# Spline coefficients on GpSimd, gathers at other places of its queue, one convolution tap on ScalarE, and two buffers for the feed block's input

## The reference

```python
xn = layernorm(x)
q = silu(causal_conv4(xn @ Wq)); k = silu(causal_conv4(xn @ Wk)); v = silu(causal_conv4(xn @ Wv))
beta = sigmoid(xn @ Wb); g = -exp(A_log) * softplus(xn @ Wa + dt_bias)
# 6 heads, keys of 64, values of 128; q and k are l2-normed
for t in tokens:
    S = S * exp(g[t]); delta = (v[t] - k[t] @ S) * beta[t]
    S = S + outer(k[t], delta); o[t] = q[t] @ S
attn = (o * rsqrt(mean(o*o) + eps) * norm_weight * silu(xn @ Wg)) @ Wo
gate_w, up_w, down_w = (catmull_rom(control_points, ...) for each)   # 2048x512, 2048x512, 512x2048
ffn = (silu(xn @ gate_w.T) * (xn @ up_w.T)) @ down_w.T
out = x + attn + ffn
```

## Time and profile before

| | |
|---|---|
| span of the profiled execution | 890.5 us |
| mean granted TensorE clock | 0.944 |
| busy: PE / DVE / ACT / POOL | 781.9 / 585.2 / 470.9 / 358.4 us |
| share of the span | 88% / 66% / 53% / 40% |
| DMA | 62.22 MB, mean 70 GB/s |

### The profile page before, as it was taken

The page is one execution under the profiler, slowest core; times in us unless marked ns, Lnnn a source line. Parts: engine busy times, 40 slices in busy tenths (PEclk is TensorE's granted clock), DMA queues, the critical chain, the costliest instruction groups (busy, mean ns, idle before and its releaser), DMA issues. The chain is left out here.

```text
span 890.5 us, 15471 instructions
## 1 busy us (share of the span) xinstructions
PE 781.9 (88%) x5688; PEld 454.6 (51%) x5688; DVE 585.2 (66%) x1425; ACT 470.9 (53%) x1078; POOL 358.4 (40%) x384
## 2 busy tenths in 40 slices
PE   2979388895988999997899997898687999999998
PEld 1455166553635774655675654664233444444443
DVE  4799958757894787796778897566593444444400
ACT  3756746462685565486666487566672333333300
POOL 3385911365795554667364768022231000000000
PEclk9989699898997999899999999999699999999999
DMA  6502010141003123003013001054695232231011
GB/s 197 198 13 51 13 61 10 65 118 37 7 1 93 45 85 94 13 1 115 7 60 112 25 1 33 6 162 104 169 186 153 72 94 85 60 82 48 25 52 44
DMA packets 60081, 62.22 MB, mean 70 GB/s; under 512 B 30535, under 2 KB 45244, under 8 KB 60006
## 3 DMA queue, kind: packets, MB, share of 16 engines
q1 hardware_dynamic: 53526, 44.97, 18.0%
q0 software_dynamic: 4224, 13.11, 5.0%
q10 hardware_dynamic: 2256, 3.15, 1.0%
HBM read 33.69 MB, written 19.73 MB: 60 GB/s over the span
## 5 line engine op out<-in xcount | busy, mean ns | idle before, releaser
L581 PE MATMUL bank<-x_parts,w 128*128 128x512 f16 x576 | 130.1, 384 | 1.5 <-DVE x_parts L942 1.5
L1971 DVE TENSOR_TENSOR hh<-sg,pu 128x512 f32<-128x512 f32 x64 | 43.9, 686 | 96.8 <-ACT sg L1942 78.8
L581 PEld LDWEIGHTS bank<-x_parts,w 128*128 128x128 f16 x576 | 56.2, 99 | 69.8 <-issue 7.0
L1863 POOL DMA_DIRECT2D yr<-y_attn x16 | 8.7, 544 | 186.7 <-DMA out<-yr 186.7
L581 PE MATMUL bank<-w,x_parts 128*128 128x384 f16 x384 | 75.7, 354 | 8.5 <-ACT V L1359 6.0
L1942 ACT ACTIVATE sg<-pg 128x512 f32<-128x512 f32 x64 | 38.0, 594 | 77.7 <-PE pg L1894 77.1
L581 PEld LDWEIGHTS bank<-w,x_parts 128*128 128x128 f16 x384 | 38.7, 106 | 39.3 <-issue 8.8
L1568 POOL TENSOR_TENSOR rn<-t,mhalf 128x6 f32<-128x6 f32 x16 | 22.7, 1417 | 89.1 <-DVE t L1148 89.1
L985 DVE SCALAR_TENSOR_TENSOR cv<-raw,taps,cv 128x512 f32<-128x512 f32 x72 | 55.1, 832 | 0.0
L1907 PE MATMUL pd<-dw,it 128*128 128x512 f16 x128 | 48.8, 381 | 0.0
L1908 PE MATMUL pd<-dw,it 128*128 128x512 f16 x128 | 48.6, 380 | 0.0
(11 more groups left out here) (293 smaller groups left out, 2050.1 us busy)
## 6 DMA issues: line engine op xcount, KB each, us to landing
xb<-in_x SPq DMA_DIRECT2D x4, 1024.0 KB
xr<-in_x SPq DMA_DIRECT2D x16, 256.0 KB, 2.6
y_attn<-xr SPq DMA_DIRECT2D x16, 256.0 KB, 2.0
down_rows<-inv SPq DMA_DIRECT2D x8, 512.0 KB
yr<-y_attn POOLq DMA_DIRECT2D x16, 256.0 KB, 2.9
out<-yr SPq DMA_DIRECT2D x16, 256.0 KB, 2.7
xn_hi<-x_parts POOLq DMA_DIRECT2D x4, 512.0 KB
xn_lo<-x_parts POOLq DMA_DIRECT2D x4, 512.0 KB
```

The costliest lines, as they stand in the source:

```text
L581: ins = nc.tensor.matmul(out, a, b, start=first and i == 0, stop=last and i == 2)
L1971: v.tensor_tensor(hh[:, i % 2, :], sg[:, i % 2, :], pu[i % 2][:], ALU.mult).then_inc(h_ready, 1)
```

## The change

The arithmetic stays the same; engines and places in their queues change.

- `Cubics` on DVE becomes `PoolCubics` on POOL: 30 linked steps and a last one, since POOL has only operations with two tensors here, so a factor is a tensor or a sum. They stand behind the W copies of supertile 0. (The old class stays for the down weights' coefficients.)
- The 16 gathers: of those in the q/k part of supertile 1 none is left; 0 to 7 stand beside the recurrence of supertile 0 and directly behind it, 8 to 15 behind the W copies of supertile 1 (before: 12 to 15), each waiting for the one before. SP's stores move with them.
- The present tap of q and k (the fourth) becomes an ACT operation (`present_tap`) that starts `cv`; DVE adds the other three.
- For supertiles 1 to 3 POOL clears `tin`, ahead of nk, and DVE no longer does.
- In the tail, `project_out` of the last chunk stands behind feature 5 instead of ahead of it, and `og_part` ahead of `turned_low`.
- x of the feed block has two places. x(1) is loaded ahead of the last move, x(2) at the block's start, x(3) behind the moves of the first supertile.

```diff
+    def slopes(self, pool):
...
+        link(pool, tt(out=self.frac[:, 1, :], in0=self.frac[:, 0, :], in1=self.one, op=ALU.subtract))
+        link(pool, tt(out=t1, in0=p1, in1=p2, op=ALU.subtract))
+        link(pool, tt(out=t2, in0=p3, in1=p0, op=ALU.subtract))
+        link(pool, tt(out=t2, in0=t2, in1=half, op=ALU.mult))
...
+    def shifted(self, pool):
...
+        link(pool, tt(out=t1, in0=c3, in1=self.u, op=ALU.mult))
+        link(pool, tt(out=t2, in0=t1, in1=t1, op=ALU.add))
...
+        g.tensor_copy(d3, c3).then_inc(self.step, 1)
...
-            ready(pe, ("WO", NCH - 2), b)
-            project_out(b, NCH - 1)
             start.features(pe, s0, 5, bank[1])
             ready(pe, ("AU", NCH - 1, 1), b)
             start.turn(pe, 2, bank[6], P.ident)
+            ready(pe, ("WO", NCH - 2), b)
+            project_out(b, NCH - 1)
...
-                for i in range(TAPS):
+                for i in range(TAPS - 1):
...
-                            if not (s.first() and n < 2):
-                                dve.wait_ge(silu_done, s.val(NBLK, n - 1))
-                        src = raw[:, n % 3, i:i + ST]
-                        out = cv[:, n % 2, :]
-                        w = P.taps[:, n, i:i + 1]
-                        if i == 0:
-                            ins = v.tensor_scalar(out, src, w, None, ALU.mult)
+                            dve.wait_ge(last_tap, s.val(NQK, n + 1))
                         else:
                             dve.wait_ge(dve_step, last[n])
-                            ins = v.scalar_tensor_tensor(out=out, in0=src, scalar=w, in1=out, op0=ALU.mult, op1=ALU.add)
...
-                if not s.first():
-                    dve.wait_ge(downs.down_stored, 32 * s.idx())
-                if s.idx() >= 2:
-                    dve.wait_ge(samples.kept, 16 * (s.idx() - 1))
-                dve.wait_ge(t32_step, step(v.memset(tin, 0.0)))
-                cleared = step(v.memset(tin[:, 0:SUB * SUB:SUB + 1], 1.0))
...
-                if b.first() and c == 0:
-                    dve.wait_ge(samples.ctrl_in, 48)
-                    samples.cubics.slopes(dve)
-                if b.first() and c == 1:
-                    samples.cubics.shifted(dve)
...
+                og_part(b, NCH - 1)
                 start.turned_low(dve, 0, bank[4])
-                og_part(b, NCH - 1)
                 start.feature_lo(dve, s0, 4, bank[0])
                 start.turned_low(dve, 1, bank[5])
-                residual(b, NCH - 1)
                 start.feature_lo(dve, s0, 5, bank[1])
                 start.turned_low(dve, 2, bank[6])
+                residual(b, NCH - 1)
...
+            def present_tap(s, n):
+
+                ready(act, ("blk", n), s)
+                if s.first() and n == 0:
+                    act.wait_ge(prep.small_in, prep.SMALL)
+                if not (s.first() and n < 2):
+                    act.wait_ge(silu_done, s.val(NBLK, n - 1))
+                sc.activation(cv[:, n % 2, :], raw[:, n % 3, TAPS - 1:], ACT.Copy, scale=P.taps[:, n, TAPS - 1:TAPS]
+                              ).then_inc(last_tap, 1)
...
                 for n in range(NQK):
                     raw_out(s, n)
+                    if n < 2:
+                        present_tap(s, n)
...
                     if n >= 2:
                         silu(s, n - 2)
+                        present_tap(s, n)
...
+                if not s.first():
+                    pool.wait_ge(downs.down_stored, 32 * s.idx())
+                    if s.idx() >= 2:
+                        pool.wait_ge(samples.kept, 16 * (s.idx() - 1))
+                    g_.memset(tin, 0.0).then_inc(tin_cleared, 1)
+                    pool.wait_ge(tin_cleared, s.val(2, 1))
+                    g_.memset(tin[:, 0:SUB * SUB:SUB + 1], 1.0).then_inc(tin_cleared, 1)
...
+                if s.first():
+                    pool.wait_ge(samples.ctrl_in, 48)
+                    samples.cubics.slopes(pool)
+                    samples.cubics.shifted(pool)
                 if s.idx() == 1:
-                    samples.gather(pool, range(12, IB), paced=True)
+                    samples.gather(pool, range(8, IB), paced=True)
...
                 if b.first():
-                    if c == NCH - 1:
-                        samples.gather(pool, range(1, 3))
+                    if c >= 1:
+                        samples.gather(pool, range(2 * c - 1, 2 * c))
...
                 norm_scale(b, 0)
+                if r == 0:
+                    samples.gather(pool, range(0, 1))
                 for c in range(1, NCH - 1):
                     beside(b, c)
                     norm_scale(b, c)
-                if r == 0:
-                    samples.gather(pool, range(0, 1))
+                    if r == 0:
+                        samples.gather(pool, range(2 * c, 2 * c + 1))
                 spill(s)
                 beside(b, NCH - 1)
                 norm_scale(b, NCH - 1)
                 pool.wait_ge(og_ready, b.val(NCH, NCH))
                 downs.low(pool, NCH * b.idx() + NCH - 1)
                 if r == 0:
-                    samples.gather(pool, range(3, 4))
+                    samples.gather(pool, range(6, 8))
...
-                if r == 0:
-                    samples.store_rows(sp)
+                    if r == 0 and c == 0:
+                        samples.store_rows(sp)
+                        samples.group(sp, range(0, 1))
                 for c in range(NCH - 2):
+                    if r == 0:
+                        samples.group(sp, range(2 * c + 1, 2 * c + 3))
                     store_y(b, c)
                     load_residual(b, c + 2)
...
-            for n in range(5, NP):
+            for n in range(5, NP - 1):
                 start.move(sp, s0, n)
+            start.load_x(sp, At(None, 1))
+            start.move(sp, s0, NP - 1)
...
-            start.load_x(sp, At(None, 1))
+            start.load_x(sp, At(None, 2))
...
-                if s < nst - 2:
-                    start.load_x(sp, At(None, s + 2))
+                if s < nst - 3:
+                    start.load_x(sp, At(None, s + 3))
...
-        if not s.first():
-            sp.wait_ge(self.feat_made, s.val(NP, 0))
-        sp.dma_start(self.x_hi.rearrange("p b c -> p (b c)"), self.scr.xh[s.idx()]).then_inc(self.x_in, 16)
-        sp.dma_start(self.x_lo.rearrange("p b c -> p (b c)"), self.scr.xl[s.idx()]).then_inc(self.x_in, 16)
+        if s.idx() == 1:
+            sp.wait_ge(self.turned_made, self.TURNS)
+        elif s.idx() >= 2:
+            sp.wait_ge(self.feat_made, s.val(NP, 0) - NP)
```

117 lines of the change are left out of this document (84 added, 33 removed).

## The result

Over 20 executions each, the kernel before takes a median of 899.5 us and the changed one 893.0, which is 6.5 less. The ratio of the two is given as 0.9905, with a 95% interval of 0.988 to 0.993, a gain of 8.5 us: it goes by executions in the chip's faster state alone, and leaves out four of the changed kernel. Forecast were 872 and a gain of 21.7. The kernel is faster, as forecast, but gains far less, and 893.0 lies above the range of 861 to 885.

What follows compares the result with a forecast made beforehand. PE was taken as the busiest engine, held up by others in the long stretches. Terms -7.8 - 6.7 + 7.9 - 5.2 + 0 - 2.2 - 7.7 = -21.7 from 892.5 gave 870.8, plus 1.2 towards the median: 872, range 861 to 885.

Steps and rivals of the forecast that it cites:

- Bound and reading: Whole kernel: PE busiest but held up by others in the long stretches; total built on the profiled execution of 892.5 us.
- Coefficients, -7.8: Recurrence beside supertile 0: cubic coefficients moved from DVE to POOL at 0.72 a step save 7.8 us net.
- the 1.9 for a late rn: Recurrence beside supertile 0: rn, queued behind POOL's coefficient steps, is done at 144.3 instead of 142.4, giving 1.9 us back.
- the "about 45": Recurrence beside supertile 0: the changed profile would show it at about 45 us, DVE waiting 2 for rn of chunk 0.
- Gathers out of the q/k part, and taps there, -8.0: Supertile 1's q/k part: removing POOL's gathers saves 6.7 us net, the present tap on ScalarE 1.3.
- Eight gathers, +7.9: Behind supertile 1's W copies: four more gathers, 2.73 us each, make the rows late, costing 7.9 us after 3.0 of slack.
- Present tap, -5.2: q/k parts of four supertiles: the tap moved from DVE to ScalarE saves 1.3 us each, 5.2 in all.
- rival 4: Supertile 0's solve and recurrence: POOL and DVE hold each other up, 0.7 per POOL operation, +20 us, total 892; 10%.
- Clearing on POOL, 0: Inversion's matrix cleared by POOL instead of DVE: 0 us, or +1.6 if POOL's pause before block 6's halo is gone.
- tail, -2.2: Attention's tail: og_part earlier and feature 5 ahead of the product save 2.2 us, half of 4.3, since moves may delay feature 6.
- Two places for x, -7.7: Feed: PE's three waits for x and 1.6 us of half clock go, 9.1 less 1.4, saving 7.7 us.
- "I leave 1.4 for them": Feed: allowance of 1.4 us, out of 9.1, for down-row gathers that POOL still issues while PE waits for x.

Runs made afterwards that it cites:

- e3: Changed kernel with feed's x(2) and x(3) loaded behind moves 2 and 3 of a supertile instead of ahead of them: median 889.2 us.
- e7: Changed kernel with feed's loads of x back in their old places, the two places kept: median 889.8 us, ratio 0.9895 to the kernel before.
- e9: Changed kernel with POOL's first v tap sum in supertile 0 held until VectorE's down-weight coefficient steps are done: median 887.0 us.
- e4: Changed kernel with the present tap of q and k back on VectorE: median 894.2 us, ratio 0.9905 to the kernel before.
- e2: Changed kernel with gathers 8 to 11 taken back ahead of the masks of chunks 2 and 3 in supertile 1: median 879.9 us.
- e12: Changed kernel with the edits of e2, e9 and e3 and four down gathers under way in feed: median 871.6 us, ratio 0.963 to the kernel before.
- e5: Kernel before, unaltered, profiled a second time in a single execution: 906.6 us, span 904.6.

## Why the prediction was wrong, point by point

- **Bound and reading.** Right for the stretches it named: both irregular ones are gone. Wrong in its base: one execution, of 892.5, was taken for the kernel, and its median of three moved the time by 1.2. The median of 20 is 7.0 above it. With the forecast's own terms 878 would have come out of the right level, which is still 15 too low.
- **Coefficients, -7.8.** Right in mechanism and step price (0.61 to 0.74 against 0.72). The stage gained 11.5 on the mean of the two executions before, and the clock in it rose from 0.84 and 0.90 to 1.00. That the 1.9 for a late rn did not come back is luck: the inversion was late for another reason (below), which gave POOL 1.7 of slack. Where the recurrence could start at 129.6 to 130.9 (e3, e7, e9; 134.8 and 136.0 in the changed kernel's own executions), DVE waits 1.1 to 1.6 behind POOL's steps and the recurrence takes 45.2 to 45.7, the "about 45" of the forecast.
- **Gathers out of the q/k part, and taps there, -8.0.** -9.0 measured; e4 gives the tap 2.1 of it, so the gathers 6.9. (The forecast's 7.8 less 1.0 is 6.8, not the 6.7 it has.)
- **Eight gathers, +7.9.** The mechanism was right and shown by e2; from the inversion on, the stage lost 9.4 on the mean of both executions before, 11.5 on the one used. In parts: the rows came 30.7 behind the last W copy where the terms give 29.4, rn began 9.2 later than before (37.7 behind that copy, 28.5 before), and 2.3 more went behind it, at half clock (288.8 to 305.9), which the term had in its bound only.
- **Present tap, -5.2.** The q/k parts gained as forecast (1.9 in supertile 0, 2.1, 1.0, 1.0). The step that failed is that the gain would shift along behind it. In supertile 0 it ran into a chain on DVE that starts when its data lands (73.5 to 73.9 in every execution, whatever came before), so at least the 1.9 was given back. And POOL's v taps, which come earlier too, meet that chain: five and seven of its steps were held in the two executions, one and four in the kernel before, some 1.0 each, and the stage is 5.2 longer on the means of two. Over nine executions of this code it is 3.3 longer, with one to seven held steps. That held steps delay the inversion is shown (it follows the chain's end by 3.2 throughout, and e9 and e12 have no held step); that the tap makes them more frequent is only likely. It is rival 4's mechanism, at a place and from a part that the prediction had not looked at; at the place it named, three short sums on DVE were held and nothing else.
- **Clearing on POOL, 0; tail, -2.2.** The way into feed is 2.4 shorter; ACT waits 2.62 for a move ahead of feature 6, the tile it has to wait for, as the prediction has it. Of what was changed on the way into feed only x(1) was tried alone (e7: it gives nothing there), and the clearing not at all.
- **Two places for x, -7.7.** The step that failed, and the largest: "I leave 1.4 for them". The three waits for x went, but the down gathers behind them came even later: feed's supertiles 0 to 2 gained nothing (158.0 before and 160.2 changed, on the means of two), and e7 without the early loads is no slower. The rows that would have told it were there, in the kernel before:

```profile
637.16 1.09 POOL L1867 DMA_INDIRECT dw<-down_rows,member  x1 [22.65 <-DMA member<-in_member]
...
673.71 0.94 POOL L1867 DMA_INDIRECT dw<-down_rows,member  x1 [1.69 <-DMA dw<-down_rows,member]
...
679.53 0.38 PE L1907 MATMUL pd<-dw,it 128*128 128x512 f16 x1
```

  The 16 gathers start one in 2.4 us, and the last is issued at 673.7, behind the end of PE's wait for x at 672.9. Such a last gather lands 3.3 to 3.6 behind its issue in e5 and e7, so here near 677.2, an estimate, and the product that needs it runs at 679.53. That leaves 2.3 of the 7.4 that the forecast takes away ahead of this place (1.06, 4.78 and 1.6), even if the gathers stay where they are. They did not: the early loads of x stand in front of the list of rows and between the gathers. What PE waits for next has to be dated, not given an allowance.

Together, by the means of two executions: -11.5 coefficients, -9.0 and +9.4 for the gathers, -1.9 and +5.2 in supertile 0, -2.0 in the q/k parts of 2 and 3, -2.4 at the seam, +2.2 in feed, +2.4 between inversion and recurrence of 2 and 3, where the clock differs from one execution to the next: -7.6, beside -7.4 between the same four executions and a measured gain of 8.5.

## What to carry to other kernels

Before a wait is costed as gained, date what its engine needs next: where a second stream lands within a few us of the first, the gain is the distance between the two and no more. A step that is moved to an idle engine, or forward in time, is to be held against everything that runs beside it at the new time. And one profile is one draw: where the granted clock differs between executions, the length of a stage is only good to some us, and the time of one execution is no base for a total.

## What the runs showed of the hardware

- In the coefficient chain of supertile 0 a VectorE step from SBUF to SBUF that meets a GpSimd operation on SBUF tiles isn't slowed down but waits for its end: a step of 0.23 to 0.29 takes 1.25 to 1.40, and ends 0.08 to 0.15 behind the other. Longer steps end later behind it (one of 0.43 by 0.28, one of 0.69 by 0.55), as if each ran only then. The Trainium skill (SBUF — State Buffer, section "SBUF: two separate sides") calls the ports between them an exclusive lock; the rows agree, also for a copy with one input (81.59). Of VectorE's operations beside the 31 GpSimd steps those that read PSUM took what they take alone (a copy of 32x192 0.35 to 0.36, as before); three sums of 4 columns in SBUF took 0.30 to 0.58 instead of 0.16.
- The same instructions take 884 to 900 us. In the changed kernel's executions time goes with the mean granted clock: 884.0 at 0.951, 899.8 at 0.928. The clock falls to 1.2 GHz after stretches in which PE is idle (in the changed kernel PE is busy for 0.81 of 3 us from 401 on and for 0.47 of the next 3, and 407 to 410 runs at half clock), and whether this catches a serial stretch such as `solve` differs by execution: the way from inversion to recurrence in supertile 3 took 49.7 and 46.6 in two executions of the same program.
- The indirect gathers of the down rows go at one in 2.6 us with two under way (38.2 us from the first to the last of 16), and at one in 1.7 with four (25.5 us), where the DMA engines' share is 1. The gathers of coefficient rows, one under way, go at one in 2.7.
